# Three softmax attentions in a decoder: GpSimd issues the next block of keys at the head of every pair, and the norm's statistics move one pair earlier

## The reference

```python
x = x + _L0_attn_ref(_layernorm(x), w_qkv, w_proj, b_proj)             # "self0"
x = x + _L0_xattn_ref(_layernorm(x), ctx, ctx, Wq, bq, Wk, bk, ...)    # "cross0"
...
x = x + _L1_xattn_ref(_layernorm(x), ctx, ctx, mask, W_o)              # "cross1"
```

## Time and profile before

| what | value |
| --- | --- |
| time, median of 3 runs | 3409.09 us (3404.37 to 3411.16) |
| the profiled execution | 3410.8 us, span 3409.0 us |
| PE busy | 2751.7 us, 81% of the span |
| DVE busy | 1918.8 us, 56% |
| POOL busy | 1430.0 us, 42% |
| ACT busy | 1341.0 us, 39% |
| mean granted clock of PE | 0.89 |

### The profile page before, as it was taken

The page is one execution under the profiler, slowest core; times in us unless marked ns, Lnnn a source line. Parts: engine busy times, 40 slices in busy tenths (PEclk is TensorE's granted clock), DMA queues, the critical chain, the costliest instruction groups (busy, mean ns, idle before and its releaser), DMA issues. The chain is left out here.

```text
span 3409.0 us, 72953 instructions
## 1 busy us (share of the span) xinstructions
PE 2751.7 (81%) x28239; PEld 1917.3 (56%) x28239; DVE 1918.8 (56%) x4178; ACT 1341.0 (39%) x2280; POOL 1430.0 (42%) x1553
## 2 busy tenths in 40 slices
PE   7977765998999989786788888794777999993394
PEld 4654444995677745564233333353446888872393
DVE  4654455115776746633588888645565666644123
ACT  3432224441111124221676776352233665650253
POOL 5644443222221155253587787534462211204555
PEclk8987786998999989797899999995788999995697
DMA  6000003640000010034000000000000000001375
GB/s 232 2 1 1 1 1 84 176 139 8 3 3 2 3 46 14 19 101 120 0 1 1 0 1 1 1 1 1 1 2 11 8 5 9 2 2 47 93 231 158
DMA packets 98053, 130.50 MB, mean 38 GB/s; under 512 B 31088, under 2 KB 76528, under 8 KB 97264
## 3 DMA queue, kind: packets, MB, share of 16 engines
q1 hardware_dynamic: 82768, 109.30, 10.7%
q0 software_dynamic: 7168, 14.78, 1.2%
q10 hardware_dynamic: 7776, 1.77, 0.2%
HBM read 103.64 MB, written 25.35 MB: 38 GB/s over the span
## 5 line engine op out<-in xcount | busy, mean ns | idle before, releaser
L672 POOL TENSOR_SCALAR arena<-arena 128x4 f32<-128x4 f32 x120 | 27.5, 229 | 1015.7 <-DVE arena L664 764.8
L2696 POOL TENSOR_TENSOR arena<-arena 128x512 f32<-128x512 f32 x256 | 318.4, 1271 | 121.9 <-ACT arena L2623 120.7
L2759 DVE TENSOR_TENSOR_SCAN arena<-ps,arena 128x512 f32<-128x512 f32 x256 | 311.8, 1218 | 58.2 <-ACT ps L2634 37.8
L2499 PE MATMUL ps<-arena,const_w 128*128 128x512 f32 x512 | 273.6, 617 | 12.9 <-DVE arena L2767 11.9
L163 PEld LDWEIGHTS ps<-L_attn_w,arena 128*128 128x128 f32 x1984 | 244.1, 195 | 52.9 <-issue 42.0
L163 PE MATMUL ps<-L_attn_w,arena 128*128 128x128 f32 x1984 | 260.3, 282 | 8.0 <-POOL arena L2709 3.4
L2634 ACT ACTIVATE ps<-arena,aneg 128x504 f32<-128x504 f32 x256 | 174.3, 681 | 102.6 <-DVE arena L2759 102.4
L435 ACT ACTIVATE arena<-ps 128x1024 f32<-128x1024 f32 x96 | 98.3, 1024 | 227.4 <-PE ps L337 227.4
L1825 PE MATMUL ps<-arena,L_attn_w 128*128 128x512 f32 x384 | 183.4, 614 | 0.9 <-ACT arena L753 0.9
L1893 ACT ACTIVATE arena<-ps,L_attn_w 128x512 f32<-128x512 f32 x64 | 44.0, 687 | 331.5 <-PE ps L1825 331.5
L318 PE MATMUL ps<-arena 64*64 64x512 f32 x768 | 122.2, 712 | 64.1 <-POOL arena L491 64.1
(11 more groups left out here) (458 smaller groups left out, 6614.2 us busy)
## 6 DMA issues: line engine op xcount, KB each, us to landing
arena<-zone_w SPq DMA_DIRECT2D x54, 512.0 KB
arena<-pair_w SPq DMA_DIRECT2D x40, 578.0 KB
arena<-rt SPq DMA_DIRECT2D x24, 384.0 KB
pair_in<-pair_free SPq DMA_DIRECT2D x1, 5200.0 KB, 37.8
arena<-pair_in SPq DMA_DIRECT2D x40, 130.0 KB
arena<-ctx SPq DMA_DIRECT2D x16, 256.0 KB, 4.6
arena<-pair_out SPq DMA_DIRECT2D x16, 256.0 KB, 5.3
arena<-arena SPq DMA_DIRECT2D x108, 32.0 KB
```

Source lines behind the costliest of these rows:

```text
L2499: pe.matmul(acc(c), e.ident, hc(m, c), start=(k == 0), stop=(k == N - 1)).then_inc(s["acc_mm"], 1)
L2696: q.tensor_tensor(bu(m, c), du(g, c), bs(m), ALU.mult).then_inc(s["bu_done"], 1)
L2759: v.tensor_tensor_scan(hs(m, c), at(c), bu(m, c), 0.0, ALU.mult, ALU.add).then_inc(s["hs_done"], 1)
```

## The change

In POOL's loop `blocks(i + 2)` is issued first in each pair, ahead of the rotation's sums and the mask; in cross0 the norm of g + 2 is issued in pair 3 instead of pair 2, behind that pair's block. In DVE's loop the statistics of g + 2 move from pair 2 to pair 1 in self0 and cross1, behind the copy of `v0`; in cross0 they stay.

```diff
             for i in range(n):
                 g, j = i // NT, i % NT
+                if i + 2 < n:
+                    blocks(i + 2)
                 if rope and g + 1 < NG and j == 0:
                     rotated(g + 1, k(g + 1), 0)
...
                 if j == 1:
                     masks(g + 1)
-                if i + 2 < n:
-                    blocks(i + 2)
-                if j == 2:
+                if j == (3 if rope else 2):
                     normed(g + 2)
                 if j == 3:
                     biased(g)
...
                     if not rope:
                         take_values("v0", g + 1)
+                        if g + 2 < NG:
+                            stats(g + 2)
                 if j == 2:
                     if rope:
                         take_values("v0", g + 1)
                     take_values("v1", g + 1)
-                    if g + 2 < NG:
+                    if rope and g + 2 < NG:
                         stats(g + 2)
```

## The result

| | before | changed |
| --- | --- | --- |
| median | 3408.6 us (3404.4 to 3411.2, 4 runs) | 3310.0 us (3307.0 to 3314.1, 4 runs) |
| ratio | | 0.9713, 95% interval 0.9697 to 0.9729 |
| profiled span | 3409.0 us | 3312.1 us |

What follows compares the result with a forecast made beforehand. PE was taken to bound self0 and cross1, while in cross0 no engine filled the time and PE waited for POOL's blocks. Gains of 84+7+6 = 97 us gave 3312 us, range 3298 to 3340.

Steps and rivals of the forecast that it cites:

- What bounds it, and what goes: cross0: PE waits for POOL's late blocks; blocks issued first remove all three waits, 2.54+3.23+1.60 = 7.37 us a group.
- The slow spells: cross0: matmuls up to twice as long behind each block wait, at 1.2 GHz; 4.77 us a group, taken as gone.
- The clock rival: cross0: remaining waits (0.5 and 1.11) may still lower PE's clock; one spell a group 11.5 us, 3324; two, 3335; chance 0.18.
- What is late next: cross0, pair 2: a new 0.5 us wait before the second values matmul; the 1.11 for the exponential stays; full group 22.4.
- the roughest term: cross0: the first group, its first block behind norm(1), taken as 24 us.
- cross0's 84: cross0: seven groups were to take 157.3 us against 241.64, a gain of 84 us.
- self0 and cross1: Statistics a pair sooner remove block waits but add 1.20 and 0.77 before the output's transposes; gains 7 and 6 us.
- The half that I took back of the slow groups: self0 and cross1: half the extra time of groups slower than the steady ones was to go, 3.4 and 2.6 us.
- The move of the waits to DVE: Bank 7's hand-overs could keep half the spells; 3.7+2.4 us a group come back, 43 over seven: about 3355; chance 0.09.
- Slower: cross0: blocks at the head delay sums by up to 1.90 us and none of the 84 comes: 3450; chance 0.02.
- the prediction's measure: cross0: POOL's idle time before the sum, 6.83 us, falling under 1.90 would decide for the slower outcome.

Runs made afterwards that it cites:

- e1: The changed kernel with GpSimd's new order alone, VectorE's statistics back in pair 2 in all three stages: 3329.4 us (ratio 0.9761).
- e3: The changed kernel, but cross0's norm is issued in pair 2 again, ahead of the block of pair 3: 3323.5 us (ratio 0.9741).
- e4: The changed kernel, but in cross0 the block of pair 1 alone is issued behind the rotation's sum of q again: 3343.8 us (ratio 0.9805).
- e8: The kernel before, with 6, 8 and 10 unneeded identity matmuls on PE ahead of cross0's three waits for a block: 3374.0 us (ratio 0.991).
- e7: The kernel before, with 12, 16 and 20 unneeded identity matmuls on PE ahead of cross0's three waits for a block: 3407.1 us (ratio 0.9997).
- e5: The changed kernel, but in self0 and cross1 the statistics stand ahead of the copy of v0 in pair 1: 3295.1 us (ratio 0.9676).

## Why the prediction was right

**What bounds it, and what goes** held as written: all three waits of a steady group of cross0 for a block vanish, by POOL's order alone (e1). For two of them the reason given is shown (e3 and e4 bring back one each, at 1.60 and 3.23, to the hundredth); the one of 2.54, with its block behind the sum of k, was not brought back alone.

**The slow spells** were taken as gone, and are, except one that runs from the end of the first group into the second (both at clock 0.92), behind a wait of 2.27 for the exponential. That they cost 4.77 a group is shown by e8. The clock rival thus fails in its size (0.88 and 24.27-22.39 = 1.9 us, once, not seven times). But its condition was not as far off as it looks. The prediction argued from a self0 group that short waits bring no spell; e3 agrees, and e7, where 1.11 alone is followed by one in four groups of five, does not. That this term came out is in part luck: which short wait lowers the clock stays open. The Trainium skill (TensorE: Matmul & The Clock Gate, HAM oscillation) tells of a kernel that starts every tile cold, with a wait for DMA of 3 to 5 us in each tile. The waits in the groups here are mostly shorter (3.23 at most), so e3 is no case against it; but here the clock fell behind waits of 1.60 and 1.11 (e7) too.

**What is late next** came out as worked out: 0.51 for 0.5, the 1.11 stays, 22.4 for 22.4. The first group took 24.45 for the 24 that was called the roughest term. cross0's 84 are 82 over the seven groups (241.64 against 159.45, from 229.60 to 389.05), and 80 for the stage: its start, before the first group, ran 2.4 us longer, with more of its projections at the lower clock.

**self0 and cross1**: the exchange of waits was right (1.60 and 0.19 against 1.27; 1.25 against 0.62), groups of 20.45 and 21.14 for 20.6 and 21.2. The half that I took back of the slow groups was too little: there are none left in steady groups of either, and so 9 and 10 us for 7 and 6. Why they all go, when PE still waits 1.27 us where it waited 1.60, no run shows. These 6 us and the 4 too many in cross0 cancel in the total, which is closer than its terms: that is luck.

**The other rivals.** The move of the waits to DVE did not happen: POOL idles 2.3 and 2.7 us before the sums, DVE has its own gaps of 1.35. *Slower* would have needed a block that is not through when DVE's rotation is. POOL's idle time before the two sums fell from 5.59 and 6.83 to 2.27 and 2.70. The block that now stands ahead took 1.90 of it; the rest is lost because a faster PE brings the sums closer together. On the prediction's measure (idle time with the block counted in, against 1.90) 4.2 and 4.6 are left, so this was nearer than the old trace let me see, but not near. Blocks beside more DVE work take 1.89 to 1.91 us still. The contention that the Trainium skill (GPSIMD Engine Reference, 8. Key points) names for DVE instructions with two SBUF inputs is not put to a test by this: in the group of cross0 looked at above, no DVE instruction reads two tensors from SBUF; each reads PSUM or a single tensor.

## What to carry to other kernels

On an engine that issues in order, put first what has long been free to run, and behind it what waits for another engine: blocks of 1.9 us behind waits of 5.6 to 6.8 were worth 80 us here. Price a wait on PE with the slow matmuls behind it, but as a range: waits of 1.11 and 1.60 were followed by a slow spell in the earlier trace rows and e7 and by none in e3 and e8, so the length of the wait alone does not tell. Where work has to be moved forward on a busy engine, look for the place where that engine idles: statistics one copy earlier (e5) turned an exchange of waits into a gain of 12 us more in the two stages.

## What the runs showed of the hardware

In cross0 of the kernel before, the scores behind the wait of 1.60 us took 1.8 to 2.0 us in all six groups, about twice their 1.09, and the granted clock was 0.53 from 411.20 to 413.40 us. In four of these groups the wait before it was 1.11. The same pair, 1.11 and 1.60, stood ahead of scores of 1.09 in five groups of e3. A wait of 3.23 brought a slow spell each time in e4, 1.6 us dear in the group shown. A wait of 1.11 was followed by transposes of 1.83 to 1.97 us in four groups of e7, whose other waits were filled with matmuls, and by transposes of 1.09 in all of e8's.

A matmul of 128x128 in float32 with nothing but the identity took 0.23 us a piece (12 in 2.84 us), while the transposes by the identity, whose 4 took 0.66 us, come at some 0.13 to 0.16. The trace shows two records for each of the former and one for each of the latter; why is not shown.
